# Re-ordering the preparation work around the key projections of a cross-attention + FFN kernel on one core

## The reference, cut to what matters

```python
# x, ctx: [8, 128, 512] fp32; mask: [8, 128, 128] int; 32 query heads, 8 key/value heads, D = 128
def reference(x, ctx, pos, mask, Wq, Wk, Wv, Wo, router_w, router_b, expert_bias):
    xn = layernorm(x)
    q = rope(split_heads(xn @ Wq, 32), pos)          # [8, 32, 128, 128]
    k = rope(split_heads(ctx @ Wk, 8), pos)          # each shared by 4 query heads
    v = split_heads(ctx @ Wv, 8)
    s = where(mask == 0, -1e9, q @ k.T / sqrt(128))
    x = x + merge_heads(softmax(s) @ v) @ Wo         # [8, 128, 4096] @ [4096, 512]
    # FFN: 64 experts, top 8 of a softmax over router logits
    h = layernorm(x).reshape(1024, 512)
    w, idx = top_k(softmax(h @ router_w.T + router_b), 8)
    out = h * w.sum(-1) + scatter(w, idx) @ expert_bias
    return x + out
```

## Time and profile before

| what | value |
|---|---|
| median of 3 runs | 584.74 us |
| the profiled execution's own time | 584.78 us |
| its span | 582.9 us (1.9 us lie outside the span) |
| PE busy | 574.8 us (99%) |
| PE idle, 0 to 20 us | 1.65 us |
| PE idle, 20 to 100 us | 0.00 us |
| PE idle, 100 to 143 us | 2.37 us |
| PE idle, 143 to 575 us | 0.38 us |
| PE idle, 575 to 582.9 us (tail) | 3.74 us |
| DVE, ACT, POOL busy | 81%, 69%, 74% |
| TensorE clock granted | 1.00 throughout (the upper level, 2.4 GHz) |

### The profile page before, as it was taken

How to read it: one execution, slowest core, us unless ns; L and a number is a source line. 1 busy time by engine, 2 the same in 40 slices (tenths; PEclk the granted TensorE clock), 3 DMA queues, 4 the chain that set the end, 5 groups by cost and what they waited for, 6 DMA issues and landing times.

```text
span 582.9 us, 10561 instructions
## 1 busy us (share of the span) xinstructions
PE 574.8 (99%) x2975; PEld 486.7 (83%) x2975; DVE 474.4 (81%) x762; ACT 402.5 (69%) x1070; POOL 432.1 (74%) x404
## 2 busy tenths in 40 slices
PE   9999999999999999999999999999999999999997
PEld 7888888777888888888888888888888888888885
DVE  5879797799897779877987798779877986797986
ACT  6356655797877767767776777777776776586655
POOL 5677699798986878688868886788678865446554
PEclk9999999999999999999999999999999999999999
DMA  8992526113301210121112111211122011100012
GB/s 286 380 310 78 164 93 218 37 37 100 100 19 56 91 55 22 53 90 54 36 36 90 54 54 22 86 54 54 37 71 70 2 56 54 37 20 1 19 38 91
DMA packets 31920, 46.95 MB, mean 81 GB/s; under 512 B 3089, under 2 KB 11665, under 8 KB 31889
## 3 DMA queue, kind: packets, MB, share of 16 engines
q1 hardware_dynamic: 31200, 45.66, 24.6%
q0 software_dynamic: 256, 0.52, 0.2%
q10 hardware_dynamic: 432, 0.40, 0.2%
HBM read 36.61 MB, written 9.96 MB: 80 GB/s over the span
## 4 chain that ended last, share of the span: by engine, by line
PE 89%; DVE 4%; issue 3%; ACT 2%; POOL 1%; DVEq 0%; ACTq 0%
PE score L1876 9%; PE outp L1900 9%; PE outp L1904 9%; PE outp L1908 8%; PE bank_a L1755 4%; PE bank_a L1757 4%; PE bank_a L1756 4%; PE probT L1955 4%; PE attnT L1741 2%; PE attnT L1743 2%; PE attnT L1742 2%; PE bank_c L1756 2%; PE bank_c L1757 2%; PE bank_c L1755 2%; PE bank_a L1741 1%
## 5 line engine op out<-in xcount | busy, mean ns | idle before, releaser
L548 POOL TENSOR_TENSOR rot<-rot,sinT 128x512 f32<-128x512 f32 x75 | 103.0, 1375 | 44.5 <-ACT rot L833 44.4
L996 ACT ACTIVATE probs<-score,negmax 128x128 f32<-128x128 f32 x256 | 90.7, 366 | 31.4 <-DVE negmax L1409 31.4
L667 POOL TENSOR_TENSOR probs<-probs,rsum 128x512 f32<-128x512 f32 x62 | 67.2, 1084 | 43.5 <-DVE rsum L1415 43.5
L1900 PE MATMUL outp<-wo_hi,oT_hi 128*128 128x512 f32 x240 | 94.9, 397 | 0.3 <-DVE wo_lo L1477 0.2
L1904 PE MATMUL outp<-wo_lo,oT_hi 128*128 128x512 f32 x240 | 93.5, 391 | 0.4 <-POOL wo_lo L553 0.4
L1908 PE MATMUL outp<-wo_hi,oT_lo 128*128 128x512 f32 x240 | 83.4, 389 | 0.0
L1422 DVE TENSOR_TENSOR resid<-resid,outp 128x512 f32<-128x512 f32 x60 | 40.9, 682 | 47.7 <-PE outp L1908 45.8
L1876 PEld LDWEIGHTS score<-kT,qT 128*128 128x128 f32 x512 | 66.8, 191 | 4.9
L1248 DVE TENSOR_TENSOR qT<-qT,rot 128x512 f32<-128x512 f32 x57 | 68.0, 1196 | 2.9 <-POOL rot L548 0.5
L1005 ACT ACTIVATE pT_hi<-probT 128x512 fp32r<-128x512 f32 x64 | 38.4, 599 | 42.1 <-PE probT L1955 41.6
L1876 PE MATMUL score<-kT,qT 128*128 128x128 f32 x512 | 67.4, 274 | 0.0
(11 more groups left out here) (361 smaller groups left out, 1523.1 us busy)
## 6 DMA issues: line engine op xcount, KB each, us to landing
ring_b<-in_wo SPq DMA_DIRECT2D x32, 256.0 KB, 3.0
ring_a<-in_wq SPq DMA_DIRECT2D x28, 256.0 KB, 2.8
v_dram<-v_stage SPq DMA_DIRECT2D x16, 256.0 KB, 5.5
v_raw<-v_dram SPq DMA_DIRECT2D x16, 256.0 KB, 2.6
k_dram<-k_stage SPq DMA_DIRECT2D x14, 256.0 KB, 2.1
kT<-k_dram SPq DMA_DIRECT2D x14, 256.0 KB, 3.0
ctx_in<-in_ctx SPq DMA_DIRECT2D x8, 256.0 KB, 6.8
ring_b<-in_wv SPq DMA_DIRECT2D x8, 256.0 KB, 7.6
```

Of the source, the lines that this page charges most:

```text
L548: pool.tensor_tensor(rot_of(k0), rot_of(k0), sinT[:, half * W:(half + 1) * W], ALU.mult).then_inc(sin_done, 1)
L667: pool.tensor_tensor(probs[:, p], probs[:, p], rsum[:, p, :].unsqueeze(2).broadcast_to([P, GH, S]), ALU.mult).then_inc(soft_done, 1)
L996: last = act.activation(probs[:, p, h, :], heads(score[p][:, :])[:, h, :], ACT.Exp, bias=negmax[:, p, h:h + 1], accum_out=sums[:, p, h:h + 1])
L1900: pe.matmul(ps[:, :], oT_hi[:, cols], wo_hi[:, h, :], start=h == 0, stop=False)
```

## The change

`mask_in` moves to the bytes of the two `rot` buffers. Its DMA moves on SP from before the x loads to behind the sixth `store_v`; the DVE instruction that reads it moves from behind the seventh value copy to behind `lo_wk(0)`; POOL's wait for `mask_done` goes, and ACT waits for it once ahead of the first key swap, which is the first to write `rot`. The load of pair 1's weights moves on SP from behind the third `store_v` to behind the first. The last two key-weight loads move behind `store_k(2)` and `store_k(3)`.

POOL does pair 0's weight sums (four instructions) and the lo parts of its W0 and W3 ahead of the first key's rope instead of between the ropes of tiles 1 to 5; W1 and W2 follow at tiles 3 and 5 instead of 7 and 8. ACT does `hi_w` of W0 and W3 ahead of the key ropes, of W1 and W2 at tiles 1 and 3 instead of 6; `hi_wk(4)` to `hi_wk(7)` go to tiles 0, 2, 4, 6. DVE does all seven `lo_x` of the second half at tiles 0, 1, 3, 5, 7, 9, 10 and `lo_wk(4)` to `lo_wk(7)` at tiles 2, 4, 6, 8; before, five of those `lo_x` and two `lo_wk` stood ahead of the first key, and two of each between the keys.

On ACT after the keys, `keep_t(0)` goes ahead of `swap_c11(1)`, and `keep_u(1)` goes ahead of `swap_c22(0)`. No arithmetic and no instruction is added or taken away.

```diff
-        mask_in = at("mask_in", [B, S], I32, 52)
+        mask_in = at("mask_in", [B, S], I32, 202)
@@ SP
             load_x(1)
-            sp.dma_start(mask_in[:, :, :], mask).then_inc(dma_mask, 16)
             load_xt(0)
             for i in range(KB * B):
                 store_v(i)
+                if i == 0:
+                    load_pair(1, 0)
                 if i == 1:
                     load_xt(1)
-                if i == 2:
-                    load_pair(1, 0)
                 if i == 4:
                     for r in range(RA):
                         load_wk(r)
+                if i == 5:
+                    sp.dma_start(mask_in[:, :, :], mask).then_inc(dma_mask, 16)
                 if i == 6:
                     sp.wait_ge(b_lo, KB * C)
                     load_pair(0, 0)
-                if 9 <= i < 9 + KV - RA:
+                if 9 <= i < 9 + WK - RA:
                     load_wk(RA + i - 9)
...
                 store_k(k)
+                if k in (2, 3):
+                    load_wk(WK + k - 2)
@@ POOL
-            pool.wait_ge(mask_done, 1)
             pool.wait_ge(table_ps, NH)
             sum_x(0)
             lo_w(W1, 1, 0)
             lo_w(W2, 1, 0)
             sum_x(1)
+            sums12(0, 0)
+            sum3(0, 0)
+            sum4(0, 0)
+            lo_w(W0, 0, 0)
+            lo_w(W3, 0, 0)
...
                 rotate((k, 0, 0), half)
-                if k == 1:
-                    sums12(0, 0)
-                if k == 2:
-                    lo_w(W0, 0, 0)
-                if k == 4:
-                    sum3(0, 0)
-                    sum4(0, 0)
+                if k == 3:
+                    lo_w(W1, 0, 0)
                 if k == 5:
-                    lo_w(W3, 0, 0)
-                if k == 7:
-                    lo_w(W1, 0, 0)
-                if k == 8:
                     lo_w(W2, 0, 0)
@@ ACT
             copy_values(V_ACT + 3)
+            copy_values(V_ACT + 4)
             for i in (T1, T2, T3, T4):
                 hi_x(i, 1)
-            hi_wk(4)
-            copy_values(V_ACT + 4)
+            copy_values(V_ACT + 5)
+            hi_w(W0, 0, 0)
+            hi_w(W3, 0, 0)
             act.wait_ge(a_lo, PIECES)
-            hi_wk(5)
-            copy_values(V_ACT + 5)
+            act.wait_ge(mask_done, 1)
...
                 swap_halves(early_bank(U_K + k)[:, :], k)
-                if k == 0:
-                    hi_w(W0, 0, 0)
-                    hi_w(W3, 0, 0)
-                if k in (3, 5):
-                    hi_wk(WK + k // 2 - 1)
-                if k == 6:
+                if k in (0, 2, 4, 6):
+                    hi_wk(RB + k // 2)
+                if k == 1:
                     hi_w(W1, 0, 0)
+                if k == 3:
                     hi_w(W2, 0, 0)
...
             swap_c11(0, KK, 0)
+            keep_t(0, 0)
             swap_c11(1, KK + 1, 0)
-            keep_t(0, 0)
             keep_t(1, 0)
             hi_v(0, 0)
             hi_wo(0, 0)
             hi_wo(0, 1)
             keep_u(0, 0)
+            keep_u(1, 0)
             swap_c22(0, KK + 2, 0)
-            keep_u(1, 0)
@@ DVE
+            LO_X = 0, 1, 3, 5, 7, 9, 10
...
-                if i == 6:
-                    dve.wait_ge(dma_mask, 16)
-                    dve.tensor_scalar(mask_bias[:, :, :], mask_in[:, :, :], 0.0, MASKED, ALU.is_equal, ALU.mult).then_inc(mask_done, 1)
...
             lo_wk(0)
+            dve.wait_ge(dma_mask, 16)
+            dve.tensor_scalar(mask_bias[:, :, :], mask_in[:, :, :], 0.0, MASKED, ALU.is_equal, ALU.mult).then_inc(mask_done, 1)
             lo_wk(1)
...
             lo_wk(3)
-            for i in range(3):
-                lo_x(i, 1)
-            lo_wk(4)
-            for i in range(3, 5):
-                lo_x(i, 1)
-            lo_wk(5)
...
                 ahead = dst
-                if k in (2, 3):
-                    lo_x(k + 3, 1)
-                if k in (5, 7):
-                    lo_wk(WK + k // 2 - 2)
+                if k in (2, 4, 6, 8):
+                    lo_wk(RB + k // 2 - 1)
+                if k in LO_X:
+                    lo_x(LO_X.index(k), 1)
```

## The result

The changed kernel takes 585.89 us (median of 15 runs, 584.86 to 586.65) against 584.7 us for the kernel before, run beside it (15 runs, 584.25 to 586.04): a ratio of 1.0018, interval 1.0012 to 1.0025 (the two medians alone would give 1.0020). That is 1.05 us slower (0.0018 x 584.7), just inside the 0.2% that the prediction called no change, and inside its range; but the forecast was +0.1, and the interval excludes it.

What follows compares the result with a forecast made beforehand. Bound: PE's waits after 100 us, above all the chain of ropes across ACT, POOL and DVE. The 1.25 us won return before the scores and at m7(2): 584.78 becomes 584.85 profiled, 584.8 us median; range 583.2 to 586.2.

Steps and rivals of the forecast that it cites:

- PE's two waits of 1.25 us: PE at m7(0) (0.38 us) and m4(1) (0.87 us), waiting for kept copies on ACT; both were to go.
- waits came back before the scores: PE before the first scores, whose ropes come no sooner: 0.8 of the 1.25 us given back, the rest at m7(2).
- the slower rival (DVE behind): DVE's list between tiles 0 and 10 lags 8.7 us, 6.0 allowed; PE waits 2.7 us, 587.5 us; chance 0.15.
- its estimate: First c11 after the key ropes, with pair 0's sums moved ahead of them: made at 101 to 102.5 us, before 102.53.
- The moves of the mask and of the key weights: Later loads in the key stage: mask cost 0 (bounds -0.2 and +0.5), key weights 6 and 7 cost 0, up to +1.
- the part on `keep_u(1)`: ACT's copy ahead of `swap_c22(0)`: m4(1)'s 0.87 us wait goes, the chain of ropes starts 0.04 to 0.12 us later.
- one or two of them falling otherwise: Five DVE or POOL instructions in the rope chain, 0.5 us each by what meets what; gives 584.8 -0.9 / +0.9.
- A second term: Sums, subtractions, mask and loads: no gain for PE, since an earlier c22 is waited away in ACT's list.
- the chain moves too: Rope chain after 100 us: lighter POOL and DVE load shortens links, scores up to 1.6 us sooner, 583.4 us; chance 0.21.

Runs made afterwards that it cites:

- the versions with the rotate held: POOL's rotate of KK+3 made to wait for the add of KK+2, in the changed kernel (584.78 us) and in the kernel before plus both copy moves (585.22 us).
- the copies alone: The kernel before with only the moves of `keep_t(0)` and `keep_u(1)`: 586.26 us, ratio 1.0028.
- with `keep_u(1)` back: The changed kernel with only `keep_u(1)` put back behind the c22 swap of pair 0: 583.88 us, ratio 0.9983.

## Why the prediction was right or wrong

Right were these. PE's two waits of 1.25 us went, and waits came back before the scores (0.66 us; 0.6 to 0.8 was said) and, smaller than forecast, at m7(2) (0.21; 0.4 to 0.5 was said). The c22 swap was forecast 0.04 to 0.12 us later and came 0.11 later (T0 + 14.42 against 14.31): what an earlier c22 gains is waited away behind `keep_u(1)`. The key stage kept PE full, with eleven DVE instructions spread over it, so the slower rival (DVE behind) did not come about. The c11 came inside its estimate (100.26 + 1.04 = 101.3; 101 to 102.5 was said). The moves of the mask and of the key weights show no price.

Wrong was one step, in the part on `keep_u(1)`: "its links (rotate, add, swap, rotate, adds) are the same instructions with the same neighbours". They are the same instructions, but not with the same neighbours. I had taken `keep_u(1)` out from between the two swaps and followed its price for the swap behind it, the c22 swap, and not for the one that it had kept apart from it: the swap of KK+3 moved up against the c22 swap, POOL got its next rotate before the last was done, and the add came to stand behind it. The sum's term for the add was 0.69 us and measured 1.76, which is +1.07; the forecast of +0.1 us against the kernel before missed the measured +1.05 by about as much. The profile before held what was needed. There, the swap of KK+3 stood behind the copy of 0.6 us and ended at 114.10, about when the rotate of KK+2 did, and the add started at 114.16 with POOL's next rotate right behind it, at 114.18; an edit that takes 0.6 us from between the two swaps turns that order round. The range did allow for "one or two of them falling otherwise", +0.9; that was this, and it should have been the forecast and not its margin. That the time still lies inside the range is owed to that margin, not to the mechanism.

From this comes a wait that I did not name, at m1(2), by which PE loses the time one product group earlier than the scores. By my own test (m7(2) more than 0.5 us from 123.2) the forecast of the mechanism failed: with the start made equal it was at 124.34. The row as it stands, 123.30, would have passed, but only by the luck of an early start. PE's idle time from 100 to 143 us, said to stay near 2.4, was 3.16.

A second term was priced at nothing and is worth 1.5 us (0.9 to 2.0): all of the change but the two copies. In the change as it was made, the price of nothing was right, since the c22 swap waits for `keep_u(1)` however early c22 is. But the prediction did not ask what the same edits give without the two copies, where the earlier c11 goes through to the scores. That the c11 is earlier because the sums left POOL's key stage is argued from POOL's load (21.63 us against 29.92) and not shown: alone the sums won nothing in the time. The rival "the chain moves too" had the size (583.4; measured 583.35 in the version without the copies) by luck and for the wrong reason: not the links became shorter, the chain began sooner.

That a rotate and an add exclude each other is what the Trainium skill's page "SBUF — State Buffer" says in its section "Who interferes with whom": a DVE instruction with two SBUF inputs contends with a GpSimd one that reads SBUF, the pair of ports that they share is an exclusive lock, and the order of issue decides who blocks. The trace agrees: the add takes 0.69 us ahead of the rotate and 1.76 behind it, and the DVE instructions with one input in PSUM stay at 0.68 to 0.69 beside the rotates (111.97 in the rows of after).

What stays open: which of the other edits makes the 1.5 us, and why the start T0 scatters. Also, the versions with the rotate held differ from each other by more (584.78 and 585.22, ratios 0.9998 and 1.0005, from two series) than their chains do, but their intervals overlap.

## What to carry to other kernels

When an instruction is moved in one engine's list, look at both its old neighbours: what stood behind it now comes earlier, and on a shared port that may put a third engine's instruction ahead of the one on the path. Take an edit apart before you judge it: here two moved copies hid the gain of all the other edits, and the others without them are the best version. Before you compare two profiles of one span, bring them to a common instruction; a start that scatters by 1 us is as large as the effects that are looked for.

## What the runs showed of the hardware

The order of a rotate on POOL and an add on DVE is settled by some hundredths of a microsecond. Read one by one, POOL's rotate of KK+3 starts 0.07 us ahead of the add of KK+2 in after (113.17 against 113.24) and 0.08 ahead in the copies alone (114.54 against 114.62), and the add takes 1.76 us; it starts 0.02 us behind the add in the kernel before (114.18 against 114.16) and with `keep_u(1)` back (113.19 against 113.17), and the add takes 0.69. The add waits for a semaphore that the rotate before it sets; if POOL's next rotate is already released by then, POOL was first each time that it was seen (after, and the copies alone). With the rotate later, 0.18 us behind the add in the version without the copies, or held by the added wait, the add was first and took 0.69 us as well. And a wait added to POOL made the kernel faster by 1.1 us (585.89 to 584.78): an engine that is held back at the right place can be worth more than one that runs ahead.
